# The remainders of the node parts move from VectorE to GpSimd in a three-layer graph network

## Chip, cores and metric

One core of one Trainium2 chip. The metric is the device time of one execution in microseconds (us). The engines appear in the profile as PE (TensorE, matmuls), PEld (TensorE's weight loads), DVE (VectorE), ACT (ScalarE), POOL (GpSimd) and SP (SyncE, which issues all DMAs here).

## The reference, cut to what matters

There are 128 graphs of 64 nodes with 384 features. Three graph layers follow each other (two in the first network, one in the second); each does, per graph,

```
u      = h @ h.T / sqrt(384)
delta  = softmax(u) * adj
attn   = delta / (sum(delta) + 1e-10)
ctx    = (attn above the diagonal) @ (h @ Wl.T + bl)
       + diag(attn) * (h @ Ws.T + bs)
       + (attn below the diagonal) @ (h @ Wr.T + br)
out    = relu(layernorm(ctx) * g + beta)
```

A layer norm with relu makes `h` ahead of the first and of the third layer, and `x` is added back after the second and the third one.

## The kernel before, in words

Two graphs fill the 128 partitions of a tile, and two tiles make a step, so each layer (a **phase**) has 32 steps, 96 in all. Phases 0 and 2 (first and third) are "bounded": their scores come from normalized rows, so no row maximum is taken, and the edge blocks are placed without a transpose. Phase 1 (the middle one) takes row maxima and transposes the edge blocks on TensorE. For the two bounded phases the input statistics are also computed, four steps ahead (`input_stats`, `gather_input`, `input_shift` on DVE, `input_rstd` on POOL); so they stand in all steps of a bounded phase but its last four, and in the last four of the middle phase.

All matmuls keep fp32 accuracy with rounded operands: each operand is held as a rounded part HI and a **remainder** LO (value minus HI), and three passes (HI HI, HI LO, LO HI) are summed. For the nodes of a step this goes so:

- `fill_source` (ACT, L525 with shift and scale in phases 0 and 2, L522 plain in phase 1) writes the step's rows, three steps ahead, into the one buffer `nodes`. Before it, it waits for `node_lo`, because the buffer must have been read by the remainder of two steps earlier.
- `turn_nodes` (DVE, L687) transposes blocks of `nodes` into `turned`; SP writes `turned` to DRAM (L324) and reads it back moved, again into `nodes` (L329).
- `split_nodes` on ACT (L530) rounds `nodes` into the HI half of `node_t` and signals `node_hi`.
- `split_nodes` on DVE (L691) subtracts HI from `nodes` into the LO half, 128 x 768 values, and signals `node_lo`. TensorE's scores and projections of the next step wait for it, too.

Every engine has a list of its own, written out by hand in its `body(s)`, and works it in order; semaphores tie the lists together. The parts of the lists that the change and the prediction touch:

- ACT, L603: round the next step's nodes (L530), round the right side (L577), two fills (L525 or L522), round the edges when bounded (L560), round the left side (L577), **seed the right bank of tile 1** with the bias (L571), scale the self part (L589), and so on; near its end scale the self part of tile 1 (L589) and seed the next self bank (L583), which waits for the centring L787 of tile 0.
- TensorE, L470: right projection of tile 0, weighing of the step before, left and self projections, scores of the next step, **right projection of tile 1** (which waits for the seed L571), cross parts, weighing, left and self projections. A projection is 9 matmuls (L427), a weighing 6 (L466), the scores 6 (L399), the cross parts 2 (L407).
- DVE, L807: diagonal (L740), **remainder of the next nodes (L691)**, statistics of the step before (L768), denominator, remainder of the right side (L763), moments, spread (L779), transpose (L687), remainder of the left side, remainder of the edges (L757), centring (L787), input statistics (L670), norm (L796), sums of scores (L707), residual (L805), and so on, to the centring of tile 0 (L787) and the remainder of its last side (L763).
- POOL, L941: output rstd of the step before (L918), input rstd (L912, L914), remainders of weight pieces in a few steps (L938, one or two 128 x 384 subtractions in step 1 and in the last four steps of the first two phases), and the placing of the next step's edges (L924, 128 columns, and L931, 512 columns).

Before the loop DVE also computes the remainders of the first weights (L751).

Of the kernel before, what the change touches and what calls it, by code (L numbers as in the profile page):

```python
# [32 lines left out]
F32 = mybir.dt.float32  # L33
F32R = mybir.dt.float32r
ALU = mybir.AluOpType
# [17 lines left out]
HI, LO = 0, 1  # L53
# [52 lines left out]
def pieces_of(s):  # L106

    if not isinstance(s.n, int) or s.phase + 1 == PHASES or s.g not in PIECES_IN:
        return []
    first = sum(count for g, count in PIECES_IN.items() if g < s.g)  # L110
    return [(s.phase + 1, first + i) for i in range(PIECES_IN[s.g])]
# [16 lines left out]
def adj_gnn_program(nc, x, adj, weights, vectors, identity, triangles, out):  # L128
# [6 lines left out]
    with ctx:  # L135
# [6 lines left out]
        def sem(name):  # L142
            return ctx.enter_context(nc.semaphore(name))
# [50 lines left out]
        moved_rows = nodes[:, :].rearrange("p (a n r) -> p n a r", a=QUARTERS, r=Q)  # L194
# [31 lines left out]
        node_hi = sem("node_hi")  # L226
        node_lo = sem("node_lo")
# [37 lines left out]
        def node_rows(s, part):  # L265

            return node_t[:, s.parity, :, :, part].rearrange("p k c (a r) -> p (k c) a r", r=Q)
# [395 lines left out]
        def _(dve):  # L663
# [22 lines left out]
                at_least(dve, squares_out, 16 * (s.n - 1))  # L686
                nc.vector.transpose(turned[:, :, :], source_blocks).then_inc(nodes_turned, 1)  # L687

            def split_nodes(s):
                dve.wait_ge(node_hi, s.n + 1)  # L690
                nc.vector.tensor_tensor(node_rows(s, LO), moved_rows, node_rows(s, HI).bitcast(F32), ALU.subtract).then_inc(node_lo, 1)  # L691

            def split_first_nodes(k):
                if k == 0:
                    dve.wait_ge(first_rounded, 1)
                else:
                    dve.wait_ge(node_hi, 1)
                mm = nc.vector.tensor_tensor(node_t[:, 0, k, :, LO], first_bank[k][:, 0:D].rearrange("p (c r) -> p c r", c=CH),
                                             node_t[:, 0, k, :, HI].bitcast(F32), ALU.subtract)
                if k == 1:  # L700
                    mm.then_inc(node_lo, 1)
# [28 lines left out]
            def denominator(s, k):  # L730

                dve.wait_ge(context_product, s.tile(k) + 1)
                dve.wait_ge(exp_done, 2 * s.n + 2)
                at_least(dve, den_sq_done, s.n)
                nc.vector.scalar_tensor_tensor(den[:, k:k + 1], total[:, s.parity, k:k + 1], GUARD, context_bank[k][:, D:D + 1],
                                               ALU.mult, ALU.add).then_inc(den_done, 1)

            def diagonal(s):
                dve.wait_ge(own_done, s.n + 1)
                nc.vector.tensor_reduce(diag[:, s.parity], own_edge[:, :, :], op=ALU.add, axis=AX.X).then_inc(diag_done, 1)  # L740
# [25 lines left out]
            def context_stats(s, k):  # L766
                dve.wait_ge(context_product, s.tile(k) + 1)
                nc.vector.bn_stats(stats[:, k], context_bank[k][:, 0:D]).then_inc(stats_done, 1)  # L768
# [38 lines left out]
            def body(s):  # L807
                prev, nxt, third, fourth = s.ahead(-1), s.ahead(1), s.ahead(3), s.ahead(4)
                diagonal(s)
                if nxt.exists():  # L810
                    split_nodes(nxt)
                if prev.exists():
                    context_stats(prev, 1)
                    denominator(prev, 1)
                split_side(s, 0, RIGHT)
                if prev.exists():
                    gather_moments(prev, 1)
                    squared_denominator(prev)
                    spreads(prev)
                if third.exists():  # L820
                    turn_nodes(third)
                split_side(s, 0, LEFT)
                if s.bounded:
                    split_edges(s)
                if prev.exists():
                    centre(prev, 1)
                if fourth.exists() and fourth.bounded:
                    input_stats(fourth, 0)
                    input_stats(fourth, 1)
                if prev.exists():  # L830
                    norm(prev, 0)
                if not s.bounded:
                    split_edges(s)
                if nxt.exists():
                    sum_scores(nxt)
                if nxt.exists() and not nxt.bounded:
                    row_maximum(nxt)
                    shift_scores(nxt)
                if fourth.exists() and fourth.bounded:
                    gather_input(fourth, 0)  # L840
                    gather_input(fourth, 1)
                if prev.exists() and prev.phase > 0:
                    residual(prev, 0)
                split_side(s, 1, RIGHT)
                if prev.exists():
                    norm(prev, 1)
                context_stats(s, 0)
                denominator(s, 0)
                if nxt.exists():
                    mask_edges(nxt)  # L850
                gather_moments(s, 0)
                if fourth.exists() and fourth.bounded:
                    input_shift(fourth)
                if prev.exists() and prev.phase > 0:
                    residual(prev, 1)
                centre(s, 0)
                split_side(s, 1, LEFT)
# [48 lines left out]
        @block.gpsimd  # L906
        def _(pool):
            def input_rstd(s):

                pool.wait_ge(in_stats_done, 2 * s.normal + 2)  # L910
                at_least(pool, source_ready, s.tile(0))
                nc.gpsimd.tensor_tensor(in_spread[:, :], in_moments[:, :, 1], ln_eps[:, :], ALU.add).then_inc(in_spread_done, 1)  # L912
                pool.wait_ge(in_spread_done, s.normal + 1)
                nc.gpsimd.tensor_tensor(in_rstd[:, :], in_spread[:, :], minus_half[:, :], ALU.pow).then_inc(in_rstd_done, 1)  # L914

            def output_rstd(s):
                pool.wait_ge(spread_done, s.n + 1)
                nc.gpsimd.tensor_tensor(rstd[:, :], spread[:, :], minus_half[:, :], ALU.pow).then_inc(rstd_done, 1)  # L918

            def place_edges(s):  # L920

                pool.wait_ge(edge_done, s.n + 1)
                at_least(pool, diag_done, s.n)
                nc.gpsimd.tensor_tensor(own_edge[:, :, :], edge[:, :, :], tri[:, 4:5, :].to_broadcast([P, 2, NODES]), ALU.mult)\  # L924
                  .then_inc(own_done, 1)

                if s.ahead(-1).bounded:
                    at_least(pool, attn_lo, s.n)
                else:
                    pool.wait_ge(edges_moved, s.n - PAIRS)  # L930
                nc.gpsimd.tensor_tensor(edge_block[:, :, :, :].rearrange("p k u (h j) -> p k (u h) j", h=2),  # L931
                                        edge[:, :, :].unsqueeze(2).to_broadcast([P, 2, 4, NODES]),
                                        tri[:, 0:4, :].unsqueeze(1).to_broadcast([P, 2, 4, NODES]), ALU.mult).then_inc(blocks_placed, 1)

            def split_piece(phase, i):
                n = (phase - 1) * PIECES + i
                pool.wait_ge(piece_hi, n + 1)
                nc.gpsimd.tensor_tensor(piece_part(phase, i, LO), piece[:, n % 2], piece_part(phase, i, HI).bitcast(F32),  # L938
                                        ALU.subtract).then_inc(piece_lo, 1)

            def body(s):  # L941
                prev, nxt, fourth = s.ahead(-1), s.ahead(1), s.ahead(4)
                pieces = pieces_of(s)
                if prev.exists():
                    output_rstd(prev)
                if fourth.exists() and fourth.bounded:
                    input_rstd(fourth)
                if len(pieces) > 0:
                    split_piece(*pieces[0])
                if len(pieces) > 1:  # L950
                    split_piece(*pieces[1])
                if nxt.exists():
                    place_edges(nxt)

            pool.wait_ge(consts_set, 1)
            start = Step(0, 0, 0)
            input_rstd(start)
            input_rstd(start.ahead(1))
            input_rstd(start.ahead(2))
            pool.wait_ge(triangles_in, 16)  # L960
            place_edges(start)
            input_rstd(start.ahead(3))
            walk(pool, body)
            output_rstd(Step(2, STEPS // 2 - 1, 1))

# [35 lines left out]
```

## Time and profile before

| | |
|---|---|
| median of 3 runs | 1274.93 us (1274.47 to 1275.84) |
| the profiled execution | 1274.82 us |
| its span | 1273.0 us |
| busy share of the span, PE / PEld / DVE / ACT / POOL | 97% / 96% / 83% / 65% / 26% |
| L691, the remainder on DVE | 95 instructions, 92.7 us, mean 975 ns |
| L931, the largest group on POOL | 96 instructions, 135.1 us, mean 1407 ns |

The span runs from the first to the last instruction on the chip. Busy times leave out waits, but a TensorE matmul's end is modelled, so its share says that it had matmuls under way, not that it went at its full rate. In a timeline each line begins with the start and the duration in us; brackets at its end name how long the engine had been idle and whose completion ended it.

### The profile page before, as it was taken

Reading aid. Unit: us, or ns where it says so; the run is one execution under the profiler, and the core shown is the slowest. Engines: PE = TensorE matmul, PEld = TensorE weight load, DVE = VectorE, ACT = ScalarE, POOL = GpSimd, SP = SyncE. Lnnn points to the kernel's source line nnn. Section 1 sums busy time; section 2 is a strip of 40 time slices with the busy share of each in tenths; the row PEclk is TensorE's granted clock in tenths of the full one; section 3 lists DMA queues with packets and bytes.
Section 4 is the critical chain, followed back from the end, with each engine's and each line's share of the span. In section 5 each row is a group of like instructions: output and inputs, shape, how many; then the busy total and the mean of one; then the engine's idle time right before and its main releaser. Section 6 shows DMA issues by size and latency. Waiting matters only on the chain.

```text
span 1273.0 us, 27433 instructions
## 1 busy us (share of the span) xinstructions
PE 1238.9 (97%) x7252; PEld 1217.9 (96%) x7252; DVE 1052.1 (83%) x3057; ACT 831.5 (65%) x2046; POOL 333.8 (26%) x438
## 2 busy tenths in 40 slices
PE   6999999999999999999999999999999999999997
PEld 4999999999999999999999999999999999999997
DVE  5888888888887777777788787889989898989886
ACT  5676666767677666656666666667666666666663
POOL 1322222222223222112112112243232323232321
PEclk7999999999999999999999999999999999999999
DMA  5433333232324322223222323432323232323221
GB/s 197 130 85 111 97 99 106 89 115 80 115 81 138 107 96 93 87 94 93 93 88 93 99 83 93 139 118 69 104 93 103 93 103 93 103 93 103 93 92 52
DMA packets 113331, 127.69 MB, mean 100 GB/s; under 512 B 11152, under 2 KB 100368, under 8 KB 113296
## 3 DMA queue, kind: packets, MB, share of 16 engines
q1 hardware_dynamic: 113296, 127.28, 31.7%
q8 instruction: 15, 0.25, 0.1%
q14 instruction: 20, 0.16, 0.0%
HBM read 77.30 MB, written 49.94 MB: 100 GB/s over the span
## 4 chain that ended last, share of the span: by engine, by line
PE 95%; issue 2%; DVE 1%; DMA 1%; SPq 0%; POOL 0%; ACT 0%; POOLq 0%; DVEq 0%; ACTq 0%
PE right_bank L427 24%; PE left_bank L427 23%; PE context_bank L427 23%; PE context_bank L466 17%; PE score_bank L399 5%; PE score_bank L407 1%; PE edge_bank L419 1%; DMA rows<-x 1%; DVE weight L751 0%; DMA squares<-turned 0%; DVE context L796 0%; DVE turned L687 0%; SPq L359 0%; SPq L369 0%; POOL edge_block L931 0%
## 5 line engine op out<-in xcount | busy, mean ns | idle before, releaser
L427 PE MATMUL context_bank<-weight,node_t 128*128 128x384 f32 x1728 | 345.8, 343 | 1.8 <-DVE weight L751 1.8
L427 PE MATMUL right_bank<-weight,node_t 128*128 128x384 f32 x1728 | 337.4, 340 | 3.8 <-DVE weight L751 2.7
L427 PE MATMUL left_bank<-weight,node_t 128*128 128x384 f32 x1728 | 334.9, 338 | 0.1
L427 PEld LDWEIGHTS left_bank<-weight,node_t 128*128 128x128 f32 x1728 | 306.6, 189 | 0.6 <-issue 0.6
L427 PEld LDWEIGHTS right_bank<-weight,node_t 128*128 128x128 f32 x1728 | 299.6, 189 | 7.5 <-issue 4.2
L427 PEld LDWEIGHTS context_bank<-weight,node_t 128*128 128x128 f32 x1728 | 300.6, 188 | 5.3 <-issue 2.1
L577 ACT ACTIVATE side_parts<-right_bank 128x384 fp32r<-128x384 f32 x192 | 94.4, 492 | 266.7 <-PE context_bank L466 266.6
L466 PE MATMUL context_bank<-side_parts,attn_t 128*128 128x386 f32 x1152 | 242.2, 345 | 16.2 <-issue 15.7
L466 PEld LDWEIGHTS context_bank<-side_parts,attn_t 128*128 128x128 f32 x1152 | 198.2, 189 | 23.7 <-issue 21.5
L589 ACT ACTIVATE context_bank<-context_bank,diag 128x386 f32<-128x386 f32 x192 | 106.3, 554 | 89.5 <-PE context_bank L427 85.7
L691 DVE TENSOR_TENSOR node_t<-nodes,node_t 128x768 fp32r<-128x768 f32 x95 | 92.7, 975 | 72.3 <-ACT node_t L530 72.3
L918 POOL TENSOR_TENSOR rstd<-spread,scalars 128x2 f32<-128x2 f32 x96 | 66.2, 690 | 294.1 <-DVE spread L779 294.1
L924 POOL TENSOR_TENSOR own_edge<-edge,tri 128x128 f32<-128x128 f32 x96 | 55.6, 579 | 312.7 <-DVE edge L728 312.7
L931 POOL TENSOR_TENSOR edge_block<-edge,tri 128x512 f32<-128x512 f32 x96 | 135.1, 1407 | 0.0
L763 DVE TENSOR_TENSOR side_parts<-right_bank,side_parts 128x384 fp32r<-128x384 f32 x192 | 106.9, 557 | 30.3 <-ACT side_parts L577 29.3
L787 DVE SCALAR_TENSOR_TENSOR context<-context_bank,moments,vector_rows 128x384 f32<-128x384 f32 x192 | 116.8, 608 | 2.6
L583 ACT ACTIVATE context_bank<-vector_rows 128x386 f32<-128x386 f32 x192 | 94.6, 493 | 24.7 <-DVE context L787 24.7
L768 DVE BATCH_NORM_STATS2 stats<-context_bank 128x6 f32<-128x384 f32 x192 | 107.1, 558 | 3.1 <-PE context_bank L466 3.1
L687 DVE STREAM_TRANSPOSE turned<-nodes 128x768 f32<-128x768 f32 x95 | 92.9, 978 | 18.5 <-ACT nodes L525 15.3
L763 DVE TENSOR_TENSOR side_parts<-left_bank,side_parts 128x384 fp32r<-128x384 f32 x192 | 102.6, 535 | 1.6 <-ACT side_parts L577 1.6
L525 ACT ACTIVATE nodes<-rows,in_shift,in_rstd 128x384 f32 (+1 forms) x128 | 83.5, 701 | 25.5 <-DVE node_t L691 18.0
L577 ACT ACTIVATE side_parts<-left_bank 128x384 fp32r<-128x384 f32 x192 | 91.6, 477 | 6.9 <-PE left_bank L427 6.6
(70 smaller groups left out, 1467.9 us busy)
## 6 DMA issues: line engine op xcount, KB each, us to landing
squares<-turned SPq DMA_DIRECT2D x95, 384.0 KB, 2.7
nodes<-squares SPq DMA_DIRECT2D x380, 96.0 KB, 2.2
rows<-x SPq DMA_DIRECT2D x64, 384.0 KB, 3.6
out<-rows SPq DMA_DIRECT2D x31, 384.0 KB, 2.6
adj_in<-adj SPq DMA_DIRECT2D x96, 64.0 KB, 1.9
piece<-weights SPq DMA_DIRECT2D x18, 192.0 KB, 2.5
rows<-weights SPq DMA_DIRECT2D x3, 576.0 KB, 8.3
vector_rows<-vectors SPq DMA_DIRECT2D x3, 576.0 KB, 7.3
```

Of the source, the lines that this page charges most:

```text
L427: mm = nc.tensor.matmul(bank[:, 0:D], node_t[:, s.parity, k, c, a], weight[:, s.phase % 2, w, c, b], start=False, stop=(c, a) == (CH - 1, ...
L466: mm = nc.tensor.matmul(context_bank[k][:, 0:DX], attn_t[:, a, k, triangle], side_parts[:, side, b], start=False, stop=(side == LEFT and a ...
L525: nc.scalar.activation(source[:, k:k + 1], rows[:, s.slot(k)], ACT.Relu, bias=in_shift[:, k:k + 1], scale=in_rstd[:, k:k + 1]).then_inc(so ...
L577: nc.scalar.activation(side_parts[:, side, HI, 0:D], side_bank[side][k][:, 0:D], ACT.Copy).then_inc(side_hi[side], 1)
L583: nc.scalar.activation(context_bank[k][:, 0:DX], vector_row(s.phase, ROW_SELF, 2), ACT.Copy)\
L589: nc.scalar.activation(context_bank[k][:, 0:DX], context_bank[k][:, 0:DX], ACT.Identity, scale=diag[:, s.parity, k:k + 1]).then_inc(self_s ...
L687: nc.vector.transpose(turned[:, :, :], source_blocks).then_inc(nodes_turned, 1)
L691: nc.vector.tensor_tensor(node_rows(s, LO), moved_rows, node_rows(s, HI).bitcast(F32), ALU.subtract).then_inc(node_lo, 1)
L763: nc.vector.tensor_tensor(side_parts[:, side, LO, 0:D], side_bank[side][k][:, 0:D], side_parts[:, side, HI, 0:D].bitcast(F32), ALU.subtrac ...
L768: nc.vector.bn_stats(stats[:, k], context_bank[k][:, 0:D]).then_inc(stats_done, 1)
L787: nc.vector.scalar_tensor_tensor(context[:, k], context_bank[k][:, 0:D], moments[:, k, 0:1], vector_row(s.phase, ROW_GAMMA), ALU.subtract, ...
L931: nc.gpsimd.tensor_tensor(edge_block[:, :, :, :].rearrange("p k u (h j) -> p k (u h) j", h=2), edge[:, :, :].unsqueeze(2).to_broadcast([P, ...
```

## The change

`split_nodes` is taken from the DVE program and put, with the same operands and the same semaphores, into the POOL program, where it is the first item of a step. On DVE it was the second item, after the diagonal.

```
--- before.py
+++ after.py
@@ in the VectorE program
-            def split_nodes(s):
-                dve.wait_ge(node_hi, s.n + 1)
-                nc.vector.tensor_tensor(node_rows(s, LO), moved_rows, node_rows(s, HI).bitcast(F32), ALU.subtract).then_inc(node_lo, 1)
...
             def body(s):
                 prev, nxt, third, fourth = s.ahead(-1), s.ahead(1), s.ahead(3), s.ahead(4)
                 diagonal(s)
-                if nxt.exists():
-                    split_nodes(nxt)
@@ in the GpSimd program
+            def split_nodes(s):
+                pool.wait_ge(node_hi, s.n + 1)
+                nc.gpsimd.tensor_tensor(node_rows(s, LO), moved_rows, node_rows(s, HI).bitcast(F32), ALU.subtract).then_inc(node_lo, 1)
...
             def body(s):
                 prev, nxt, fourth = s.ahead(-1), s.ahead(1), s.ahead(4)
                 pieces = pieces_of(s)
+                if nxt.exists():
+                    split_nodes(nxt)
                 if prev.exists():
                     output_rstd(prev)
```

## Rows read from the trace of the kernel before

**Rows 1.** Busy time by stretch (us, then each engine's busy us and instructions, TensorE clock)

```profile
44.00:431.00 387.00, 386.93 (x2297) 386.41 (x2295) 319.29 (x967) 267.96 (x659) 107.89 (x156) 1.00 0.34 102
904.00:1222.00 318.00, 318.00 (x1855) 312.36 (x1854) 286.82 (x852) 215.83 (x527) 93.79 (x125) 1.00 0.30 98
```

**Rows 2.** Timeline of one step of the third phase (start us, us, engine, line, what)

```profile
1104.78 1.31 ACT L525 ACTIVATE nodes<-rows,in_shift,in_rstd 128x384 f32 x2 [0.54 <-DVE node_t L691]
...
1106.23 0.98 DVE L687 STREAM_TRANSPOSE turned<-nodes 128x768 f32<-128x768 f32 x1 [0.16 <-ACT nodes L525]
...
1106.89 0.48 ACT L571 ACTIVATE right_bank<-vector_rows 128x384 f32<-128x384 f32 x1
...
1107.42 1.51 PEld L427 LDWEIGHTS right_bank<-weight,node_t 128*128 128x128 f32 x9
...
1114.33 0.61 DVE L787 SCALAR_TENSOR_TENSOR context<-context_bank,moments,vector_rows 128x384 f32<-128x384 f32 x1
...
1114.97 0.50 ACT L583 ACTIVATE context_bank<-vector_rows 128x386 f32<-128x386 f32 x1 [0.69 <-DVE context L787]
...
1115.40 0.83 ACT L530 ACTIVATE node_t<-nodes 128x768 fp32r<-128x768 f32 x1
...
1116.26 0.96 DVE L691 TENSOR_TENSOR node_t<-nodes,node_t 128x768 fp32r<-128x768 f32 x1 [0.67 <-ACT node_t L530]
...
1117.45 1.31 ACT L525 ACTIVATE nodes<-rows,in_shift,in_rstd 128x384 f32 x2 [0.55 <-DVE node_t L691]
...
1118.68 0.69 POOL L918 TENSOR_TENSOR rstd<-spread,scalars 128x2 f32<-128x2 f32 x1 [3.11 <-DVE spread L779]
```

**Rows 3.** Timeline of an ordinary step of the first phase

```profile
288.27 0.84 ACT L530 ACTIVATE node_t<-nodes 128x768 fp32r<-128x768 f32 x1
...
290.43 1.30 ACT L525 ACTIVATE nodes<-rows,in_shift,in_rstd 128x384 f32 x2
...
292.52 0.48 ACT L571 ACTIVATE right_bank<-vector_rows 128x384 f32<-128x384 f32 x1
...
293.51 1.54 PEld L427 LDWEIGHTS right_bank<-weight,node_t 128*128 128x128 f32 x9
```

**Rows 4.** Timeline of a step of the middle phase

```profile
646.36 0.49 ACT L571 ACTIVATE right_bank<-vector_rows 128x384 f32<-128x384 f32 x1
...
648.39 1.54 PEld L427 LDWEIGHTS right_bank<-weight,node_t 128*128 128x128 f32 x9
```

**Rows 5.** Lines L924 and L931: durations in ns, min/median/max, first and last start

```profile
L924 POOL TENSOR_TENSOR own_edge<-edge,tri x96: 450/467/884, 23.2 to 1252.1; 128x128 f32<-128x128 f32 x96
...
L931 POOL TENSOR_TENSOR edge_block<-edge,tri x96: 1277/1309/1685, 23.6 to 1252.9; 128x512 f32<-128x512 f32 x96
```

**Rows 6.** Timeline of a first-phase step in which weight pieces are split

```profile
398.56 0.52 ACT L595 ACTIVATE weight<-piece 128x384 fp32r<-128x384 f32 x1
...
399.15 1.03 POOL L938 TENSOR_TENSOR weight<-piece,weight 128x384 fp32r<-128x384 f32 x1 [3.30 <-ACT weight L595]
...
400.47 0.84 ACT L530 ACTIVATE node_t<-nodes 128x768 fp32r<-128x768 f32 x1
400.56 1.31 POOL L931 TENSOR_TENSOR edge_block<-edge,tri 128x512 f32<-128x512 f32 x1
...
401.34 1.34 DVE L691 TENSOR_TENSOR node_t<-nodes,node_t 128x768 fp32r<-128x768 f32 x1 [0.41 <-ACT node_t L530]
...
402.71 0.94 ACT L522 ACTIVATE nodes<-rows 128x384 f32<-128x384 f32 x2
...
404.45 0.48 ACT L571 ACTIVATE right_bank<-vector_rows 128x384 f32<-128x384 f32 x1
...
405.71 1.54 PEld L427 LDWEIGHTS right_bank<-weight,node_t 128*128 128x128 f32 x9
```

**Rows 7.** Timeline of the first step

```profile
25.95 1.49 DVE L751 TENSOR_TENSOR weight<-rows,weight 128x384 fp32r<-128x384 f32 x3
...
28.54 1.31 ACT L525 ACTIVATE nodes<-rows,in_shift,in_rstd 128x384 f32<-128x384 f32 x2 [2.26 <-DVE node_t L691]
```

## Prediction, made before the changed kernel was run

> **What bounds the kernel now.** I read the busy time by stretch first, then the timeline of one step in each phase, then the rows of GpSimd (POOL in the profile; VectorE is DVE, ScalarE is ACT). In the stretches of the first and the third phase TensorE (PE) shows busy for practically the whole time, at a granted clock of 1.00 [rows 1]. That looks like a kernel bound by PE alone, but the rate per matmul differs. A bounded step issues 74 matmuls (six projections of 9, two weighings of 6, 6 for scores, 2 for the cross parts). The first phase takes 387.00/2297 x 74 = 12.47 us a step, the third 318.00/1855 x 74 = 12.69 us [rows 1]. PE's matmul ends are modelled, so 0.22 us a step of the third phase is hidden waiting.
>
> The timeline of a third-phase step says for what. ACT's seed of the right bank (L571) runs from 1106.89 for 0.48 us, to 1107.37; PE loads its first weight for that bank at 1107.42, that is 0.05 us later [rows 2]. So PE waits for ACT there, and ACT's list can be followed back: the seed follows the two fills (L525 at 1104.78), which waited 0.54 us for the DVE remainder L691. Forward it closes into a loop: the fills release the transpose L687 (1106.23), DVE then works down its list to the centring L787 (1114.33), that releases the self seed L583 (1114.97, which waited 0.69 us for it), ACT goes on to the rounding L530 (1115.40), that releases L691 (1116.26), and this the next fills (1117.45) [rows 2]. One turn is 1117.45 - 1104.78 = 12.67 us: the third phase goes at the pace of this loop, and **the node remainder L691 is a link of it**.
>
> In the first phase the same chain has slack. The seed of the right bank ends at 292.52 + 0.48 = 293.00 and PE takes it at 293.51 [rows 3]; less the 0.05 us of hand-over, that leaves 0.46 us. In the middle phase the seed ends at 646.85 and PE takes it at 648.39, 1.49 us of slack [rows 4].
>
> **The change part by part.** It takes 95 L691 subtractions off DVE and puts them first in GpSimd's step. No DMA is added or removed.
>
> *What DVE saves* is 0.96 us a step, plus the 0.67 us that it waited for L530 [rows 2]. I cost this gain at nothing: after the split DVE only reaches the transpose L687, which waits for the fills, and the fills wait for the remainder. DVE gets to that wait earlier and stands there longer.
>
> *What the subtraction takes on GpSimd* is not in the trace. The median GpSimd tensor_tensor over 128 columns took 467 ns, over 512 columns 1309 ns [rows 5], a slope of 2.19 ns a column; for 768 columns this gives 1.309 + 256 x 0.00219 = **1.87 us** (an estimate). The 384 columns of L938, the same subtraction with the same output type, fit this line: 1.03 us by the line, 1.03 measured [rows 6]. From below: 1.309 us for the first 512 columns and DVE's 0.96/768 = 1.25 ns for each further one, 1.63 us. From above: two L938, 2.06 us. I take 1.87, on which three sizes agree.
> The Trainium skill, GPSIMD Engine Reference, section 3.1 (Elementwise), gives 4497 ns for 2048 fp32 columns, from which 768 columns would be an estimated 1.69 us; with it the sum below would come to about 1304 us. The rows speak for the longer time, since they show the fixed part too.
>
> *The hand-overs.* ACT to DVE is 1116.26 - 1116.23 = 0.03 us [rows 2]; ACT to GpSimd 399.15 - 399.08 = 0.07 us [rows 6]. From the remainder's end to the fill it is 1117.45 - 1117.22 = 0.23 us [rows 2]; from GpSimd to ACT nothing is shown, and I take the same.
>
> *GpSimd's queue.* It had been idle 3.11 us before L918 at 1118.68 [rows 2], that is from 1115.57, while L530 ends at 1116.23: the subtraction finds it free. It would end at about 1118.2, ahead of L918, so the output rstd behind it is not held up.
>
> *Third phase.* From the end of L530 to the fill: 0.07 + 1.87 + 0.23 = 2.17 us in place of 0.03 + 0.96 + 0.23 = 1.22 us, 0.95 us more in each turn of the loop. All later links hang on the fill and move with it, so nothing takes it up. The full loop (with input statistics four steps ahead) stands in 28 of the 32 steps: 28 x 0.95 = **+26.6 us**.
>
> *First phase.* L530 ends at 289.11, so the fill starts at 289.11 + 2.17 = 291.28 in place of 290.43 [rows 3]: 0.85 us late, of which 0.46 us is slack. The 0.39 us left delays PE in every step, since the next step's ACT list waits for PE. Steps 1 to 28 fill in this form: 28 x 0.39 = **+10.9 us**.
>
> TensorE's scores also wait for the remainder: they come six matmuls (6 x 12.47/74 = 1.0 us) before the right bank, at 292.5, and the subtraction would end at 289.11 + 1.94 = 291.05, so that wait stays covered.
>
> *Middle phase.* The same 0.85 us lies inside its 1.49 us of slack [rows 4]: 0. This cover goes if the subtraction took over 1.87 + 0.64 = 2.5 us.
>
> *Steps with weight pieces.* There GpSimd is busy with L931 until 400.56 + 1.31 = 401.87, later than L530's end at 401.31 [rows 6]. The subtraction would end near 403.77 and the fill start at 403.80 (L522 followed L691 by 0.03 us there) in place of 402.71: 1.09 us late, against a slack of 405.71 - 404.93 - 0.05 = 0.73 us [rows 6]. That is 0.36 us in each of two steps, and some 0.5 us where the third phase begins: **+1.2 us**.
>
> *Start.* The first fill waited 2.26 us for L691, which stood behind the weight remainders L751 on DVE [rows 7]. On GpSimd it is free of that queue, and up to 2.26 us could come back; but if the subtraction gets in between the three L751, the first self projection is late by up to its 1.87 us. I take 0.
>
> **The sum:** 26.6 + 10.9 + 1.2 = 38.7 us on the profiled execution's own 1274.82 us (span 1273.0), which stands 0.11 us under the median of the runs: **1313.5 us**. With 1.63 us for the subtraction each link is 0.24 us shorter: 28 x 0.71 + 28 x 0.15 + 0.5 - 1 = 23.6, 1298.4 us. With 2.06 us: 28 x 1.14 + 28 x 0.58 + 1.8 + 1.9 = 51.9, 1326.7 us.
>
> **The rivals.**
> *Faster: DVE is what the third phase lacks.* If DVE's own list, not the loop through the remainder, set the 12.69 us, taking 0.96 us off would bring the third phase to PE's 12.47 us: about 25 steps x 0.22 = 5.5 us, 1269.3 us. For it: DVE is busy 286.82 of 318.00 us there [rows 1], and L583 waits for DVE in the shown step. Against: in the same step DVE itself waits 0.67 us before L691 and 0.16 us before L687 [rows 2], so it isn't the one that is always late. It decides only if GpSimd's subtraction takes under 0.96 - 0.04 - 0.22 = 0.70 us, and the 512-column row alone took 1.31 us. Chance 0.05.
>
> *Only the third phase pays.* Were the fill of the first phase not tied to PE's right bank as I read it, its 10.9 us would go: 1302.6 us. For it: no PE wait is seen there; against: the order on ACT is fixed. Chance 0.12.
>
> *GpSimd and DVE hold each other up.* In a piece step L691 took 1.34 us rather than 0.96 where it started while GpSimd's L931 was running, 0.38 us more [rows 6]. If each subtraction on GpSimd were stretched so, that is 0.38 us on each link: 28 x 1.33 + 28 x 0.77 + 2.1 + 1.9 = 62.8, 1337.6 us. Against: during the subtraction DVE would run statistics, the denominator and the side remainder, which take at most one SBUF tensor, while the slowed L691 took two; and the change removes just this two-input operation. Chance 0.08.
> The Trainium skill, SBUF — State Buffer, section "Who interferes with whom", says that a DVE instruction with two SBUF inputs and a GpSimd instruction reading SBUF exclude each other, the second one waiting; the stretched L691 agrees with that.
>
> *No change to be measured.* The pieces could cancel, DVE's relief against a small first-phase cost. That needs a subtraction near 0.7 us as well. Chance 0.03.
>
> **How the numbers follow.** My forecast has 0.72. From its bounds (1298.4 and 1326.7) and the second rival (1302.6, inside) the range is 1297 to 1330 us; what lies outside is the hold-up, the gain and no change, 0.16 together. A measurement of this kernel can tell about 0.2%, 2.5 us. Faster by more than that is 0.05, within it 0.03, slower 0.92.
>
> **What would show it.** Right: a GpSimd subtraction of 1.8 to 1.95 us, x95; the wait of the fills L525 for it rising by about 0.9 us a step in the third phase; 13.6 us a step there and about 12.85 in the first phase; the middle phase within 0.05 us of before; ACT's right seed ending 0.05 us before PE's weight load in the first phase as well; DVE idle before the transpose, released by the fills. Wrong: a subtraction much off 1.87 us, a first phase that stays at 12.47 us, or a third phase whose centring comes earlier against the fills than in [rows 2], which would mean that DVE's relief is worth something after all.

## The result, and the profile after

The changed kernel takes 1315.05 us (median of 4 runs, 1314.54 to 1315.72) against 1274.72 us (median of 4): 1.0315 times the time before, with a 95% interval of 1.0297 to 1.0333. That is 40.3 us slower; the forecast was 38.7 us, 1313.5 us in a range of 1297 to 1330.

The head of the profile's page of the changed kernel (busy us, share of the span, instructions), then its busy time by stretch, answering to [rows 1]:

```profile
span 1313.0 us, 27433 instructions
...
PE 1249.6 (95%) x7252; PEld 1220.1 (93%) x7252; DVE 988.4 (75%) x2962; ACT 828.4 (63%) x2046; POOL 509.0 (39%) x533
```

```profile
44.00:431.00 387.00, 384.02 (x2239) 378.07 (x2238) 285.44 (x913) 260.50 (x645) 159.12 (x182) 1.00 0.33 99
904.00:1222.00 318.00, 297.84 (x1727) 290.69 (x1727) 259.69 (x768) 201.67 (x491) 129.76 (x140) 1.00 0.28 91
```

DVE lost 63.7 us of work (1052.1 to 988.4), POOL gained 175.2 us, and PE's share fell from 97% to 95%. By matmuls, as in the prediction, a step of the first phase now takes 387.00/2239 x 74 = 12.79 us and one of the third 318.00/1727 x 74 = 13.63 us. The starts of ACT's rounding (L530, one a step) give it more exactly; the table has the time between the second, 33rd, 65th and 95th start, and the mean step inside each phase (between the 5th and 28th, the 37th and 57th, the 72nd and 92nd start; steps of the experiments below are the same means):

| us | second start | to 33rd (first phase) | to 65th (middle) | to 95th (third) | step, first | step, middle | step, third |
|---|---|---|---|---|---|---|---|
| before | 38.44 | 386.96 | 436.65 | 379.18 | 12.467 | 13.605 | 12.701 |
| after | 40.31 | 396.77 | 438.66 | 405.49 | 12.804 | 13.597 | 13.629 |
| difference | +1.87 | +9.81 | +2.01 | +26.31 | +0.337 | -0.008 | +0.928 |

The four differences add to the 40.0 us by which the span grew. Now the timeline of a third-phase step, answering to [rows 2] (L691 has become L916 on POOL, L787 is L783, L918 is L912):

```profile
1150.03 1.32 ACT L525 ACTIVATE nodes<-rows,in_shift,in_rstd 128x384 f32 x2 [1.46 <-POOL node_t L916]
...
1151.48 0.98 DVE L687 STREAM_TRANSPOSE turned<-nodes 128x768 f32<-128x768 f32 x1 [1.46 <-ACT nodes L525]
...
1152.14 0.48 ACT L571 ACTIVATE right_bank<-vector_rows 128x384 f32<-128x384 f32 x1
...
1152.67 1.52 PEld L427 LDWEIGHTS right_bank<-weight,node_t 128*128 128x128 f32 x9 [1.05 <-ACT right_bank L571]
...
1159.65 0.60 DVE L783 SCALAR_TENSOR_TENSOR context<-context_bank,moments,vector_rows 128x384 f32<-128x384 f32 x1
...
1160.30 0.50 ACT L583 ACTIVATE context_bank<-vector_rows 128x386 f32<-128x386 f32 x1 [0.75 <-DVE context L783]
...
1160.73 0.83 ACT L530 ACTIVATE node_t<-nodes 128x768 fp32r<-128x768 f32 x1
...
1161.63 1.85 POOL L916 TENSOR_TENSOR node_t<-nodes,node_t 128x768 fp32r<-128x768 f32 x1 [0.73 <-ACT node_t L530]
...
1162.84 0.66 DVE L741 TENSOR_TENSOR den_sq<-den 128x2 f32<-128x2 f32 x1
...
1163.70 1.31 ACT L525 ACTIVATE nodes<-rows,in_shift,in_rstd 128x384 f32 x2 [1.47 <-POOL node_t L916]
1163.84 0.69 POOL L912 TENSOR_TENSOR rstd<-spread,scalars 128x2 f32<-128x2 f32 x1 [0.36 <-DVE spread L775]
```

It is the same loop, one turn in 13.67 us. From the fill to the centring it takes 1159.65 - 1150.03 = 9.62 us, before 9.55: DVE's part is no shorter. (Odd and even steps differ by about 0.07 us. Over the 20 turns between the 72nd and the 92nd start, the mean time from the end of the fills to the next rounding is 9.34 us in both kernels.) ACT rounds until 1161.56, POOL subtracts from 1161.63 for 1.85 us, and the fill follows at 1163.70, 0.22 us after. The bracket of the fill has grown from 0.54 to 1.46 us, that of the transpose from 0.16 to 1.46: ACT waits for POOL, DVE waits for ACT, and PE's weight load stood idle for 1.05 us until the seed ended, 0.05 us before it.

A first-phase step, answering to [rows 3], and a middle-phase one, answering to [rows 4]:

```profile
283.94 0.84 ACT L530 ACTIVATE node_t<-nodes 128x768 fp32r<-128x768 f32 x1
...
284.85 1.84 POOL L916 TENSOR_TENSOR node_t<-nodes,node_t 128x768 fp32r<-128x768 f32 x1 [0.71 <-ACT node_t L530]
...
286.91 1.31 ACT L525 ACTIVATE nodes<-rows,in_shift,in_rstd 128x384 f32 x2 [0.71 <-POOL node_t L916]
...
289.02 0.48 ACT L571 ACTIVATE right_bank<-vector_rows 128x384 f32<-128x384 f32 x1
...
289.55 1.51 PEld L427 LDWEIGHTS right_bank<-weight,node_t 128*128 128x128 f32 x9 [0.30 <-ACT right_bank L571]
```

```profile
655.42 1.84 POOL L916 TENSOR_TENSOR node_t<-nodes,node_t 128x768 fp32r<-128x768 f32 x1 [0.31 <-ACT node_t L530]
...
657.41 0.94 ACT L522 ACTIVATE nodes<-rows 128x384 f32 x2 [0.64 <-POOL node_t L916]
...
658.63 0.48 ACT L571 ACTIVATE right_bank<-vector_rows 128x384 f32<-128x384 f32 x1
...
660.22 1.54 PEld L427 LDWEIGHTS right_bank<-weight,node_t 128*128 128x128 f32 x9
```

In the first phase the seed now ends at 289.50 and PE loads at 289.55: the slack of 0.46 us is used up and PE waits. In the middle phase the seed ends at 659.11 and PE comes at 660.22, 1.11 us later: less the 0.05 us of hand-over, 1.06 us of slack are left, and the step is as long as before.

The subtraction itself (durations in ns, min/median/max), and the waits of the whole kernel (who waited for whom, us in total, times, longest):

```profile
L916 POOL TENSOR_TENSOR node_t<-nodes,node_t x95: 1829/1841/2085, 26.2 to 1282.1; 128x768 fp32r<-128x768 f32 x95
```

```profile
DVE stats L764 <- PE context_bank L466: 130.4, 96, 2.4
DVE turned L687 <- ACT nodes L525: 75.6, 60, 1.5
...
ACT nodes L525 <- POOL node_t L916: 66.2, 61, 1.8
...
PEld right_bank L427 <- ACT right_bank L571: 35.2, 52, 1.1
```

### The profile page after: what moved, and what is told of

It is laid out like the page before. It is cut to its first block, busy times and chain, and to the rows that moved or that the text cites. A ratio compares the mean times of both kernels' runs of the same rounds, so it can differ in the third digit from the quotient of the medians.

```text
span 1313.0 us, 27433 instructions
## 1 busy us (share of the span) xinstructions
PE 1249.6 (95%) x7252; PEld 1220.1 (93%) x7252; DVE 988.4 (75%) x2962; ACT 828.4 (63%) x2046; POOL 509.0 (39%) x533
## 4 chain that ended last, share of the span: by engine, by line
PE 46%; issue 19%; POOL 13%; DVE 11%; ACT 7%; ACTq 1%; DMA 1%; DVEq 1%; POOLq 0%; SPq 0%
PE right_bank L427 12%; PE context_bank L427 11%; PE left_bank L427 11%; PE context_bank L466 8%; POOL node_t L916 8%; ACT nodes L525 3%; POOL edge_block L929 3%; PE score_bank L399 2%; DVE context L783 2%; DVE turned L687 2%; ACT node_t L530 2%; DVE in_stats L670 2%; POOL in_rstd L908 1%; PE edge_bank L419 1%; DVE attn_t L753 1%
## 5 line engine op out<-in xcount | busy, mean ns | idle before, releaser
L764 DVE BATCH_NORM_STATS2 stats<-context_bank 128x6 f32<-128x384 f32 x192 | 107.8, 561 | 130.4 <-PE context_bank L466 130.4
L916 POOL TENSOR_TENSOR node_t<-nodes,node_t 128x768 fp32r<-128x768 f32 x95 | 175.2, 1844 | 52.1 <-ACT node_t L530 52.1
L687 DVE STREAM_TRANSPOSE turned<-nodes 128x768 f32<-128x768 f32 x95 | 92.9, 978 | 99.5 <-ACT nodes L525 75.6
L906 POOL TENSOR_TENSOR in_spread<-in_moments,scalars 128x2 f32<-128x2 f32 x64 | 17.3, 271 | 350.8 <-DVE in_moments L675 350.8
L525 ACT ACTIVATE nodes<-rows,in_shift,in_rstd 128x384 f32 (+1 forms) x128 | 83.9, 703 | 73.0 <-POOL node_t L916 66.2
L783 DVE SCALAR_TENSOR_TENSOR context<-context_bank,moments,vector_rows 128x384 f32<-128x384 f32 x192 | 116.6, 607 | 2.6
L571 ACT ACTIVATE left_bank<-vector_rows 128x384 f32<-128x384 f32 x192 | 94.1, 490 | 0.0
```

The lines of the kernel that those rows point to most:

```text
L525: nc.scalar.activation(source[:, k:k + 1], rows[:, s.slot(k)], ACT.Relu, bias=in_shift[:, k:k + 1], scale=in_rstd[:, k:k + 1]).then_inc(so ...
L783: nc.vector.scalar_tensor_tensor(context[:, k], context_bank[k][:, 0:D], moments[:, k, 0:1], vector_row(s.phase, ROW_GAMMA), ALU.subtract, ...
L916: nc.gpsimd.tensor_tensor(node_rows(s, LO), moved_rows, node_rows(s, HI).bitcast(F32), ALU.subtract).then_inc(node_lo, 1)
```

## The experiments

**Cut the link (e1, e2).** The fills get a buffer of their own, once with the remainder on GpSimd (e1), once on VectorE (e2). For the space, the weight pieces go down to one buffer, and the second piece of a step is loaded later.

```
+        filled = sb("filled", [P, 2 * D])
...
-        source = nodes[:, :].rearrange("p (k d) -> p k d", k=2)
+        source = filled[:, :].rearrange("p (k d) -> p k d", k=2)
...
-                    act.wait_ge(node_lo, s.n - 1)
+                    act.wait_ge(nodes_turned, s.n - 1)
...
+                    sp.wait_ge(node_lo, after.n)
                     read_squares(after)
```

> The changed kernel, with the remainder on GpSimd, but the fills write a buffer of their own, so they no longer wait for the remainder (the weight pieces give up one of their two buffers for the space). Link theory (the remainder costs time only because the next fills wait for it): with the link cut, first and third phase both go at TensorE's 12.47 us a step; against the kernel before the third phase gives back 25 x 0.22 = 5.5 us and the start loses some 1.6 us: 1271 us, between 1267 and 1276. Rival, that GpSimd is simply too slow a place or holds VectorE up: the subtraction still takes 1.84 us on the same engine, so most of the 40 us stay, 1305 to 1316 us.

> The kernel before, with the remainder on VectorE, and the same buffer of their own for the fills. Link theory: the third phase goes from 12.69 to about 12.47 us a step, 1274.7 - 5.5 = 1269 us, between 1267 and 1272. Rival, that the third phase is set by VectorE's own list and not by the loop through the fills: no change, 1274 to 1276 us. If GpSimd and VectorE end within 3 us of each other once the link is cut, where the remainder runs is worth nothing off the loop.

Measured: e1 1280.13 us (ratio 1.0038, 1.0024 to 1.0052), e2 1278.98 us (1.0029, 1.0017 to 1.0042). Against the changed kernel e1 gives back 35 of the 40 us, so the rival of e1 falls. But both expected times were missed by some 9 or 10 us, and yet the steps are as the link theory has them: 12.467 us in the first phase for both, in the third 12.466 (e1) and 12.550 (e2). So with the remainder still on GpSimd the third phase loses nothing at all. What was missed is in the main a side effect of the smaller piece buffer: the last four steps of the middle phase took 63.45 us (e1) and 63.03 us (e2), 56.30 before, and the waits of e1 name why:

```profile
DVE turned L689 <- ACT filled L527: 15.5, 55, 0.3
...
ACT weight L597 <- DMA piece<-weights: 10.0, 5, 2.8
```

ACT waited 10.0 us for late pieces (in e2, too), a wait that the kernel before doesn't have, while DVE's wait for the fills ahead of the transpose, 75.6 us in the changed kernel, fell to 15.5. The last four steps account for 7 of the missed 9 or 10 us; the second step, which splits two pieces as well and where ACT waited 2.2 us for one of them, is another 1 us in both runs. In e2 the 0.08 us a step above 12.467 in the third phase are another 2; in e1 the second rounding came at 41.29 us, 1.2 us later than the 1.6 us that I had allowed for the start. The two runs end 1.2 us apart, inside the 3 us that I had set, but only because two differences nearly cancel: e1 loses 3.0 us to e2 at the start and gains 2.2 in the third phase. A step of e1's third phase, from its timeline (its buffer `filled` takes the fills):

```profile
1147.13 0.83 ACT L532 ACTIVATE node_t<-nodes 128x768 fp32r<-128x768 f32 x1
...
1148.04 1.84 POOL L918 TENSOR_TENSOR node_t<-nodes,node_t 128x768 fp32r<-128x768 f32 x1 [0.74 <-ACT node_t L532]
...
1148.97 1.30 ACT L527 ACTIVATE filled<-rows,in_shift,in_rstd 128x384 f32 x2
...
1151.07 0.49 ACT L573 ACTIVATE right_bank<-vector_rows 128x384 f32<-128x384 f32 x1
...
1152.05 1.54 PEld L431 LDWEIGHTS right_bank<-weight,node_t 128*128 128x128 f32 x9
```

The fill starts at 1148.97, in the middle of the subtraction (1148.04 to 1149.88, as long as ever), and the seed ends 0.49 us before PE comes for it.

**Half of the link (e7, e8).** To cut without touching the pieces: the buffer of two halves becomes one of three. The fills write halves 0 and 1, the moved nodes come into halves 1 and 2, and only the second fill waits for the remainder, and only the first for the shift (e7 on VectorE, e8 on GpSimd).

```
-        nodes = sb("nodes", [P, 2 * D])
+        nodes = sb("nodes", [P, 3 * D])
-        source = nodes[:, :].rearrange("p (k d) -> p k d", k=2)
+        source = nodes[:, 0:2 * D].rearrange("p (k d) -> p k d", k=2)
...
-        moved_rows = nodes[:, :].rearrange("p (a n r) -> p n a r", a=QUARTERS, r=Q)
+        moved_rows = nodes[:, D:3 * D].rearrange("p (a n r) -> p n a r", a=QUARTERS, r=Q)
...
-                    act.wait_ge(node_lo, s.n - 1)
+                    act.wait_ge(*((node_lo, s.n - 1) if k == 1 else (nodes_turned, s.n - 1)))
...
-                    act.wait_ge(in_shift_done, s.normal + 1)
+                    if k == 0:
+                        act.wait_ge(in_shift_done, s.normal + 1)
```

> The kernel before, remainder on VectorE, but the first of the two fills writes into a half of its own (the buffer of two halves becomes one of three, the fills take halves 0 and 1, the moved nodes halves 1 and 2), so that only the second fill waits for the remainder. Link theory: the first fill (0.65 us) leaves the loop, so the third phase would go at 12.70 - 0.65 us if nothing else held it; the run with the whole link cut on VectorE went at 12.55 us, so 12.47 to 12.55 us a step, 4 to 6 us less than before in all: 1269 to 1272 us, faster than both kernels. Rival, that the gain of a cut link was only argued, since the two cut kernels came out no faster than the kernel before: 1274 to 1277 us.

> The changed kernel, remainder on GpSimd, with the same three halves. Link theory: 0.65 us less in each turn of the third phase's loop, 13.63 - 0.65 = 12.98 us a step, and the first phase, late by 0.34 us a step, back to 12.47: 1315.1 - 28 x 0.65 - 28 x 0.34 = 1287 us, between 1284 and 1290. Rival, that GpSimd's place or its sharing with VectorE costs the time: 1310 to 1316 us.

Measured: e8 1284.71 us (1.0079, 1.0063 to 1.0095), steps of 12.467 and 12.948 us: the third phase's step is 0.68 us shorter than in the changed kernel, and 30 us of the 40 are back though every subtraction still runs on GpSimd. A step of its third phase:

```profile
1135.73 1.85 POOL L917 TENSOR_TENSOR node_t<-nodes,node_t 128x768 fp32r<-128x768 f32 x1 [0.74 <-ACT node_t L531]
...
1136.22 0.70 ACT L526 ACTIVATE nodes<-rows,in_shift,in_rstd 128x384 f32 x1
...
1137.71 0.71 ACT L526 ACTIVATE nodes<-rows,in_shift,in_rstd 128x384 f32 x1 [0.79 <-POOL node_t L917]
...
1139.75 1.52 PEld L427 LDWEIGHTS right_bank<-weight,node_t 128*128 128x128 f32 x9 [0.38 <-ACT right_bank L572]
```

The first fill now runs beside the subtraction; the second still waits for it, and PE still waits for the seed. The edit shortens the loop in two places. Behind the remainder stands one fill of 0.71 us in place of a pair of 1.31, which is 0.60 us (the two fills of the pair overlap by 0.10), and since the second fill no longer waits for the shift, the hand-over ahead of it fell from 0.22 to 0.14 us (means of 20 turns). Together that is 0.69 us for the 0.68 by which the step shrank.

e7 1270.90 us (0.9967, 0.9954 to 0.9979): **faster than both kernels**, by 0.3% against the kernel before, as expected, with 12.551 us a step in the third phase. What holds it there is in its timeline:

```profile
1111.50 0.60 DVE L788 SCALAR_TENSOR_TENSOR context<-context_bank,moments,vector_rows 128x384 f32<-128x384 f32 x1
...
1112.14 0.50 ACT L584 ACTIVATE context_bank<-vector_rows 128x386 f32<-128x386 f32 x1 [0.75 <-DVE context L788]
...
1112.57 0.83 ACT L531 ACTIVATE node_t<-nodes 128x768 fp32r<-128x768 f32 x1
...
1113.44 0.96 DVE L692 TENSOR_TENSOR node_t<-nodes,node_t 128x768 fp32r<-128x768 f32 x1 [0.68 <-ACT node_t L531]
...
1113.97 1.30 ACT L526 ACTIVATE nodes<-rows,in_shift,in_rstd 128x384 f32 x2
...
1115.86 0.98 DVE L688 STREAM_TRANSPOSE turned<-nodes 128x768 f32<-128x768 f32 x1
1116.06 0.49 ACT L572 ACTIVATE right_bank<-vector_rows 128x384 f32<-128x384 f32 x1
...
1117.05 1.54 PEld L427 LDWEIGHTS right_bank<-weight,node_t 128*128 128x128 f32 x9
```

The fills start at 1113.97, while the remainder still runs, and end at 1115.27; the transpose starts at 1115.86 with no wait before it. DVE now comes to it late from its own list: this is the next limit, the same 12.55 us as in e2, and there VectorE's relief is worth something (e1, which differs from e2 in the engine of the remainder, goes at 12.466).

**Refill VectorE (e3).** Against the changed kernel, two statistics whose results nobody reads.

```
                 diagonal(s)
+                if nxt.exists():
+                    for k in range(2):
+                        nc.vector.bn_stats(spare[:, k], node_t[:, s.parity, k, :, HI].bitcast(F32))
```

> The changed kernel with two 128x384 statistics of no use (about 1.1 us a step) on VectorE in the place that the remainder left, so that VectorE's relief is taken away again. Link theory, in which the relief is worth nothing: 1315 us, between 1313 and 1318. Rival, that VectorE's relief gave something back that hid a part of the cost: slower by more than that, up to 28 x 1.1 = 31 us for each phase that VectorE bounds, so 1320 us or more.

Measured: 1315.19 us (1.0315, 1.0298 to 1.0332), the changed kernel's time. DVE's busy time grew from 988.4 to 1071.7 us, and its waits show where the 83 us went:

```profile
DVE turned L688 <- ACT nodes L526: 75.6, 60, 1.5
DVE stats L765 <- PE context_bank L467: 48.2, 67, 1.6
```

The wait for PE ahead of the statistics fell from 130.4 to 48.2 us; the one ahead of the transpose stayed at 75.6. The relief was spent on waiting, as forecast.

**One phase alone (e5, e6).** Against the kernel before, the remainder goes to GpSimd only for the nodes of the third phase (e5, shown) or of the middle phase (e6); the others stay on VectorE.

```
-                if nxt.exists():
+                if nxt.exists() and not (nxt.phase == 2):
                     split_nodes(nxt)
...
+                if nxt.exists() and (nxt.phase == 2):
+                    split_nodes(nxt)
                 if prev.exists():
                     output_rstd(prev)
```

> The kernel before, with GpSimd computing the remainders of the third phase's nodes alone. Link theory: 28 x 0.93 = 26 us and up to 1 us where the phase begins: 1300 to 1303 us; first phase at 12.47 us a step, third at 13.63. Rival, a cost spread evenly over all 95 subtractions (40/95 each): 32 x 0.42 = 13.5 us, 1288 us.

> The kernel before, with GpSimd computing the remainders of the middle phase's nodes alone. Link theory: the delay lies inside the middle phase's slack; only its last steps, where GpSimd still works on weight pieces, may lose up to 2 us: 1275 to 1277.5 us. Rival, a cost spread evenly over all 95 subtractions: 13.5 us, 1288 us.

Measured: e5 1302.58 us (1.0217, 1.0201 to 1.0234), with steps of 12.467 us in the first phase and 13.635 in the third, and e6 1275.87 us (1.0008, 0.9998 to 1.0017), both inside the link theory's ranges. A third of the subtractions costs 27.6 us in one phase and under 1 us in another: the cost hangs on the slack of the phase, not on the count. In e6 the last four steps of the middle phase took 56.92 us, 0.62 more than before.

**A shorter hand-over (e4).** Against the kernel before, the two waits ahead of the fill change places.

```
+                    if s.phase != 1:
+                        act.wait_ge(in_shift_done, s.normal + 1)
                     act.wait_ge(node_lo, s.n - 1)
...
-                    act.wait_ge(in_shift_done, s.normal + 1)
+                    if isinstance(s.n, int) and s.n <= 2:
+                        act.wait_ge(in_shift_done, s.normal + 1)
```

> The kernel before, but ahead of the fill with shift and scale ScalarE waits first for the shift and then for the remainder, so that the second wait doesn't stand between the remainder's end and the fill (0.23 us there, against 0.03 us at the plain fill). Link theory: a link shortened by up to 0.2 us shortens the third phase by up to 25 x 0.2 = 5 us and leaves the first phase alone: 1270 to 1273 us. Rival, that the third phase is not set by this loop: no change, 1274 to 1276 us.

Measured: 1273.91 us (0.9991, 0.9981 to 1.0000), a miss: by its time alone it can't be told from no change. The steps say more. Over the 20 turns between the 72nd and the 92nd start the fill followed the remainder by 0.178 us on average, before by 0.226, so the link shrank by 0.048 us rather than 0.2; the third phase's step went from 12.701 to 12.654, by 0.047 us. The link theory holds, the size that I had put on the swapped wait did not.

The traces show what that size had wrong. Most steps run in a loop of the program, where the counts that a wait compares with are worked out in registers; the first two and the last four steps of a phase are written out, with plain numbers. The 0.03 us at the plain fill [rows 6] came from a written-out step. In a written-out step a fill with shift and scale, which has both waits, follows just as fast. This is one of the kernel before:

```profile
834.76 0.96 DVE L691 TENSOR_TENSOR node_t<-nodes,node_t 128x768 fp32r<-128x768 f32 x1 [0.67 <-ACT node_t L530]
...
835.75 0.71 ACT L525 ACTIVATE nodes<-rows,in_shift,in_rstd 128x384 f32<-128x384 f32 x1 [0.35 <-DVE node_t L691]
```

That is 0.03 to 0.04 us from the remainder's end to the fill, with two waits. In the looped steps of the changed kernel's middle phase the plain fill, with one wait, took 0.15 us (the subtraction's 655.42 + 1.84 to 657.41 above). So most of the 0.22 us goes with the loop, and not with the second wait.

**The start (e9).** Against the changed kernel, the remainder of step 1 alone goes back to VectorE (VectorE's list is shown, against the kernel before; the same condition, turned round, stands in GpSimd's).

```
-                if nxt.exists():
+                if nxt.exists() and not (not (isinstance(nxt.n, int) and nxt.n == 1)):
                     split_nodes(nxt)
```

> The changed kernel, but the very first remainder in the loop (the nodes of step 1) stays on VectorE, where it follows the weight remainders, in place of running on GpSimd beside them. Hold-up theory: the three weight remainders go back from 3.10 us to 1.49 us, the second rounding of nodes comes at 38.4 us from the start of the span in place of 40.3, and the time falls by 1.7 to 1.9 us: about 1313.3 us. Rival, that the late start comes from something else (the loads, TensorE's clock at the start): weight remainders and time as in the changed kernel, 1315 us.

In the changed kernel the first step reads so (first the second of the three L747 by itself, then the three merged with what follows), and in e9 so (timeline of each):

```profile
26.53 2.16 DVE L747 TENSOR_TENSOR weight<-rows,weight 128x384 fp32r<-128x384 f32 x1
...
26.06 3.10 DVE L747 TENSOR_TENSOR weight<-rows,weight 128x384 fp32r<-128x384 f32 x3
26.18 2.08 POOL L916 TENSOR_TENSOR node_t<-nodes,node_t 128x768 fp32r<-128x768 f32 x1 [0.24 <-ACT node_t L530]
...
29.30 2.34 PE L427 MATMUL context_bank<-weight,node_t 128*128 128x384 f32 x9 [4.19 <-DVE weight L747]
```

```profile
25.87 1.49 DVE L751 TENSOR_TENSOR weight<-rows,weight 128x384 fp32r<-128x384 f32 x3
...
27.47 0.95 DVE L691 TENSOR_TENSOR node_t<-nodes,node_t 128x768 fp32r<-128x768 f32 x1
...
27.50 1.81 PE L427 MATMUL context_bank<-weight,node_t 128*128 128x384 f32 x9 [2.65 <-DVE weight L751]
```

Measured: 1313.21 us (1.0299, 1.0282 to 1.0316), 1.84 us less, and the second rounding at 38.36 us. Beside the subtraction the three weight remainders L747 took 3.10 us rather than 1.49, the subtraction 2.08 rather than 1.84, and PE waited 4.19 us for the weights: the two engines did hold each other up here. The whole loss on VectorE is in the second L747, which started while the subtraction ran, took 2.16 us in place of 0.55 and ended 0.4 us after it; the first and the third took 0.55 us as ever.

## Why the prediction was right, step by step

- **The loop through the remainder** was the right reading. Three different changes of the link moved the third phase's step one to one: +0.92 us on the link (1.84 + 0.07 in place of 0.96 + 0.03) gave +0.928; the first fill and a part of the hand-over taken out (0.69) gave -0.68; 0.048 off the hand-over gave -0.047. With the whole link cut the step was 12.466, PE's own. The term of 26.6 us came to 26.3.
- **1.87 us for the subtraction** was 1.841 (median of 95). The line through 128 and 512 columns held at 768. By the Trainium skill, GPSIMD Engine Reference, section 3.1, it would have been an estimated 1.69 us; the measurement decides for the longer one.
- **The first phase**, 0.39 us a step over the slack, was 0.337; its term of 10.9 us and the 0.7 for two piece steps, together 11.6, came to 9.81. 0.03 of the 0.05 us is the shorter subtraction; where the rest comes from stays open.
- **VectorE's relief costed at nothing**: e3 shows it for the changed kernel. It holds only while the loop is the limit: with the link cut, e2 and e1 differ by 0.084 us a step of the third phase.
- **The middle phase** at 0 was right for its ordinary steps. Its last four, where GpSimd still works on weight pieces, took 57.72 us against 56.30; I had put 0.5 us there, so this term was too small by about 1 us. The whole stretch to the 65th start grew by 2.0 us, 1.5 more than forecast.
- **The start**, taken as 0 between -2.26 and +1.87, was mis-sized: +1.87, the upper end. The way there was the one named, the subtraction getting in between the three L747 (L751 before): the second of them waited it out.
- **The hold-up of GpSimd and DVE**, the third rival, did not come on the link: the subtraction took 1841 ns in the median, 1829 at the least. But the list of what DVE does beside it was not complete. The squared denominator (L741) multiplies `den` by itself, two SBUF inputs, and in 40 of its 96 instances it started while the subtraction ran. In the step shown it took 0.66 us and ended at 1163.50, just behind the subtraction's 1163.48; its median is 0.13 us, and in the kernel before none took over 0.14. This cost DVE 17 us in all and the kernel nothing in that step, because DVE then waits 1.46 us for the fills ahead of the transpose. By the Trainium skill, SBUF — State Buffer, section "Who interferes with whom", a VectorE instruction with two SBUF inputs contends with a GpSimd instruction that reads SBUF. The trace agrees in both places, the second L747 and L741; only the first is seen to have cost time.
- **The rivals.** "Only the third phase pays" falls with the 9.81 us of the first; "faster" and "no change" fall with the result, and the 0.70 us below which GpSimd would have had to stay is far from 1.84.

The errors (-0.3 in the third phase, -1.8 in the first, +1.5 in the middle one, +1.9 at the start) partly cancel: that the sum came within 2 us is in part luck, and the terms are what was tested.

## What to carry to other kernels

Before work is moved to an idle engine to relieve a busy one, look at who waits for the result: here the busy engine waited over 1 us a step anyway ((318.00 - 286.82)/25 in the third phase [rows 1]), and the moved instruction was a link of a loop, so that its longer latency was paid in each step. If an operation in a loop is slow, try first to take the wait on it away: a buffer of three halves in place of two made the kernel faster than both versions, if only by 0.3% against the kernel before. And an engine that shows itself busy for the whole of a stretch may still be waiting: the time per matmul by stretch told it.

## What the hardware showed that was not expected

A VectorE instruction with two SBUF inputs that started beside the GpSimd subtraction was not slowed in proportion: it ended only after the subtraction. The second L747 did so after 2.16 us in place of 0.55, and L741, of only 128 x 2 values, in all of the 40 instances that started beside it, each time 0.01 to 0.03 us behind the subtraction's end. The subtraction itself lost 0.24 us where it met a two-input instruction that was already running (2.08 us in the first step). Statistics and side remainders, which take at most one SBUF tensor, were not stretched beside it, nor it by them (median 1.841 us).

Wherever the fill of the changed kernel waited for the remainder, the hand-over was 0.03 to 0.04 us in the written-out steps, with one wait and with two. In the looped steps it was 0.15 us with one wait (L522, 26 steps) and 0.21 to 0.23 with two (L525, 52 steps). A second wait that had long been reached thus cost next to nothing outside the loop and some 0.05 to 0.09 us inside it, where e4 took back 0.048 us and e8 0.09.
